# Graph network layer on one core: the blend of the experts moved into the stage of the sparse table

## What is computed

```
x = x + experts(layernorm(x))          # 4 experts, gates g[node, e], two of four not zero
    # out = sum_e g[node, e] * (gelu(x @ W1[e] + b1[e]) @ W2[e] + b2[e])
y = layernorm(x)                       # mean and variance of each node's row of 256
h_self, h_neigh = y @ W_self, y @ W_neigh
h_sparse = maxk(h_neigh, 32)           # keep the 32 largest of each row, zero the rest
x = x + h_self + mean over incoming edges of h_sparse[src]
```

## Time and profile before

| what | us |
|---|---|
| median of 3 runs | 4285.53 |
| lowest and highest | 4283.12, 4290.53 |
| the profiled execution's own time | 4285.15 |
| its span in the trace | 4283.4 |
| the stage of the gates, first to last VectorE instruction | 2853.7 to 2879.7 |
| the stage of the blend | 2880.6 to 2947.9 |
| the stage of the sparse table | 2949.6 to 3138.9 |
| busy share over the span: PE, DVE, ACT, POOL | 85%, 63%, 41%, 65% |

### The profile page before, as it was taken

One profiled execution on the slowest core, in us unless ns is written; L12 is line 12 of the kernel. 1 busy time (PEld: TensorE's weight loads), 2 busy tenths in 40 slices (PEclk: granted clock), 3 DMA queues, 4 the chain that ended last, 5 costly groups with the idle time before them and its releaser, 6 DMA issues. The chain is left out here.

```text
span 4283.4 us, 74278 instructions
## 1 busy us (share of the span) xinstructions
PE 3654.7 (85%) x19739; PEld 2736.6 (64%) x19739; DVE 2717.2 (63%) x9603; ACT 1744.8 (41%) x4053; POOL 2802.9 (65%) x2913
## 2 busy tenths in 40 slices
PE   5999977777687889886899999968769999996988
PEld 2565544444455557645788888866358888885667
DVE  7866757666544444336455555568978888886862
ACT  4766644333233233324444544436523333333420
POOL 6777667777777777771777777751667767675330
PEclk9999997888899999865899999989879999998988
DMA  8665553333444443531433333346389999993001
GB/s 285 205 208 200 203 179 113 112 110 113 123 129 131 132 120 105 165 104 22 102 70 66 71 66 70 68 115 212 119 301 384 368 364 385 362 383 125 1 1 60
DMA packets 362257, 690.88 MB, mean 161 GB/s; under 512 B 70066, under 2 KB 188224, under 8 KB 355485
## 3 DMA queue, kind: packets, MB, share of 16 engines
q0 software_dynamic: 133184, 338.60, 26.8%
q1 hardware_dynamic: 228671, 347.51, 24.0%
HBM read 572.74 MB, written 113.14 MB: 160 GB/s over the span
## 5 line engine op out<-in xcount | busy, mean ns | idle before, releaser
L1199 POOL DMA_INDIRECT e_ring<-table,erow x1040 | 1001.7, 963 | 316.9 <-issue 172.2
L1650 PE MATMUL e_sums<-e_ring,e_onehot 128*128 128x257 f32 x2080 | 772.1, 476 | 297.0 <-DMA e_ring<-table,erow 250.8
L2749 POOL DMA_INDIRECT t_source<-source_rows,t_index x632 | 605.6, 958 | 206.6 <-issue 157.8
L1650 PEld LDWEIGHTS e_sums<-e_ring,e_onehot 128*128 128x128 f32 x2080 | 363.1, 216 | 528.2 <-issue 288.9
L1762 POOL DMA_INDIRECT e_ring<-table,esrc x544 | 532.4, 979 | 215.9 <-issue 124.7
L1165 ACT ACTIVATE k_sign<-ramp,low 128x128 bf16<-128x128 f32 x1024 | 361.3, 394 | 436.5 <-PE e_sums L1604 417.5
L1847 PE MATMUL e_total<-e_loads,e_times 128*128 128x256 f32 x3072 | 505.4, 301 | 21.1 <-DMA e_loads<-table 16.7
L645 POOL DMA_INDIRECT r_ring<-rows,esrc x400 | 381.2, 953 | 156.4 <-issue 77.8
L1745 ACT ACTIVATE e_times<-e_tally 128x320 fp32r<-128x320 f32 (+4 forms) x640 | 259.8, 426 | 491.4 <-PE e_tally L1831 486.5
L1847 PEld LDWEIGHTS e_total<-e_loads,e_times 128*128 128x128 f32 x3072 | 411.8, 191 | 70.1 <-issue 29.8
L2933 PE MATMUL t_raw<-big,t_w 128*128 128x256 f32 x1600 | 375.8, 389 | 19.2 <-ACT t_hidden L2768 18.6
(11 more groups left out here) (570 smaller groups left out, 6600.2 us busy)
## 6 DMA issues: line engine op xcount, KB each, us to landing
e_loads<-table SPq DMA_DIRECT2D x512, 256.0 KB
table<-stage SPq DMA_DIRECT2D x49, 1024.0 KB
outputs<-first_outputs SPq DMA_DIRECT2D x49, 512.0 KB, 6.5
first_outputs<-t_stage SPq DMA_DIRECT2D x96, 256.0 KB
t_near<-near_rows SPq DMA_DIRECT2D x79, 256.0 KB
e_ring<-table,erow POOLq DMA_INDIRECT x1040, 2.8
table<-n_split SPq DMA_DIRECT2D x49, 256.0 KB, 2.1
t_source<-source_rows,t_index POOLq DMA_INDIRECT x632, 2.5
```

Source lines behind the costliest of these rows:

```text
L1199: eng.indirect_dma_start(ring[:, t % RING, 0:D], None, table, bass.IndirectOffsetOnAxis(ap=b.erow[:, EARLY + t:EARLY + t + 1], axis=0)).th ...
L1650: eng.matmul(sums[g % SUMS][:, 0:ACCW], onehot[t % ONEHOTS][:, :], ring[:, t % RING, :], start=(t % GROUP == 0), stop=(t % GROUP == GROUP ...
L2749: eng.indirect_dma_start(source[s][:, q, :], None, a.source_rows, bass.IndirectOffsetOnAxis(ap=index[s][:, q:q + 1], axis=0)).then_inc(gat ...
```

## The change

What was the phase `blend` is done inside `sparse_table`; the phase is gone.

- The outputs of the experts land in the big buffer (10 windows instead of 13), as do the diagonal matrices (4 windows) and a new tile `raised` (2 windows). The gates' tile and the fetch semaphores belong to a larger scope, which is now a `Phase` itself, and so ends with a clearing of semaphores and a meeting of the engines.
- All four experts go through TensorE: `lay` makes four diagonal matrices on ScalarE, `blend` does four products, `lift` copies the bank to `raised` on ScalarE, `merge` adds it to the features on GpSimd.
- The first six windows are blended ahead of the first product. In round w of the sparse table stand `lay(w+9)` and `lift(w+8)` on ScalarE, `blend(w+8)` on TensorE, `merge(w+8)` on GpSimd; rounds 0 and 1 take two windows each, and from round 41 there is nothing left to blend.
- The statistics are made by groups of four windows. Groups 0 and 1 stand ahead of the search. Those of group m+2 are a generator whose steps are taken after the MATCH_REPLACE8 of the rounds 1 to 3 in the search of group m: four `bn_stats`, then three, three and one small instructions, the reciprocal, the product.
- ScalarE takes the square root of group k ahead of `norm(4k)`, and `norm(4k)` waits for that group's scale and shift.
- The big buffer is cleared in eight pieces on GpSimd, in rounds 41 to 48.
- `weigh` does two heads in each of the rounds 41 to 44, and `cooling` comes after the last full group.

The core of the diff:

```diff
-FETCHED = 13
+FETCHED = 10
...
-def blend(nc, b, a):
...
+    blended_at = [[6, 7], [8, 9]] + [[w + AHEAD] for w in range(2, NW - AHEAD)] + [[] for _ in range(AHEAD + 1)]
...
 # gpsimd
+            def merge(w):
+                eng.wait_ge(lifted, w + 1)
+                eng.tensor_tensor(b.x[:, w, :], b.x[:, w, :], raised[w % RAISED][:, :], ALU.add).then_inc(blended, 1)
...
+            for w in range(FIRST):
+                merge(w)
             for w in range(NW):
+                for ahead in blended_at[w]:
+                    merge(ahead)
+                if w >= CLEARED:
+                    empty(w - CLEARED)
                 eng.wait_ge(evacuated, w + 1)
+                eng.wait_ge(counted, w + 1)
                 eng.tensor_tensor(b.x[:, w, :], b.x[:, w, :], full[w % WAYS][:, 0, :], ALU.add).then_inc(added, 1)
                 if w >= LATER:
                     choose(w - LATER)
...
 # vector
+            def statistics(k):
+                cols = slice(GROUP4 * k, min(GROUP4 * (k + 1), NW))
...
+                for w in range(cols.start, cols.stop):
+                    eng.wait_ge(blended, w + 1)
+                    eng.bn_stats(b.counts[:, w, :], b.x[:, w, :]).then_inc(counted, 1)
+                    yield
+                eng.wait_ge(counted, cols.stop)
+                s.did(eng.tensor_tensor(work[:, 0, cols], even(1), odd(1), ALU.add))
+                s.did(eng.tensor_tensor(work[:, 1, cols], even(1), odd(1), ALU.subtract))
+                s.did(eng.tensor_tensor(work[:, 2, cols], even(2), odd(2), ALU.add))
+                yield
...
+                yield
+                s.settled()
+                s.did(eng.tensor_tensor(spread[:, cols], work[:, 2, cols], work[:, 3, cols], ALU.add))
+                yield
+                eng.wait_ge(rooted, k + 1)
+                r.did(eng.reciprocal(b.rstd[:, cols], std[:, cols]))
+                yield
+                r.settled()
+                r.did(eng.scalar_tensor_tensor(b.shift[:, cols], b.mean[:, cols], -1.0, b.rstd[:, cols], ALU.mult, ALU.mult))
...
                         eng.match_replace(left[q][:, :], best[q][:, :], values(q), TAKEN).then_inc(picked[q], 1)
+                        if r > 0:
+                            next(beside, None)
...
-                search(here(0))
+                search(here(0), statistics(2 * i + 2))
...
 # scalar
             def norm(w):
                 wait_if(eng, transposed, w - 1)
+                if w % GROUP4 == 0:
+                    eng.wait_ge(scaled, 2 * (w // GROUP4 + 1))
...
+            def lay(w):
+                wait_if(eng, summed, w - GATES + 1)
+                for e in range(EXPERTS):
+                    gate = eng.activation(gates[w % GATES][:, e, :], b.ident[:, :], ACT.Copy, scale=b.gate[:, w, e:e + 1])
+                gate.then_inc(laid, 1)
+
+            def lift(w):
+                eng.wait_ge(summed, w + 1)
+                wait_if(eng, blended, w - RAISED + 1)
+                eng.activation(raised[w % RAISED][:, :], mixed[w % BANKS][:, 0:D], ACT.Copy).then_inc(lifted, 1)
...
             for w in range(NW):
                 if w + 2 < NW:
+                    if (w + 2) % GROUP4 == 0:
+                        root((w + 2) // GROUP4)
                     norm(w + 2)
                 if w + 1 < NW:
                     copy(w + 1)
+                    for ahead in blended_at[w + 1]:
+                        lay(ahead)
                 if w >= LATER:
                     hide(w - LATER)
                 eng.wait_ge(multiplied, w + 1)
...
                                ACT.Copy).then_inc(evacuated, 1)
+                for ahead in blended_at[w]:
+                    lift(ahead)
```

More of the change, by code:

```diff
@@ L3086, in _ @@
             step(eng.reciprocal(stat[:, 1, :], stat[:, 0, :]))
-            step(eng.tensor_tensor(a.gate[:, :, :], score[:, :, :],
+            step(eng.tensor_tensor(b.gate[:, :, :], score[:, :, :],
                                    stat[:, 1, :].unsqueeze(2).broadcast_to([P, NW, EXPERTS]), ALU.mult))
-def blend(nc, b, a):
[L3099 to L3169, removed]
@@ L3221, in sparse_table @@
         work = sb("n_work", [P, 4, NW])
+        spread = sb("n_spread", [P, NW])
         std = sb("n_std", [P, NW])
@@ L3334, in search @@
                         eng.match_replace(left[q][:, :], best[q][:, :], values(q), TAKEN).then_inc(picked[q], 1)
+                        if r > 0:
+                            next(beside, None)
+                for _ in beside:
+                    pass
                 for w, q in few:
@@ L3351, in pair @@
                         head(w)
-                search(here(GROUP4))
+                search(here(GROUP4), statistics(2 * i + 3) if 2 * i + 3 <= NW // GROUP4 else iter(()))
                 for w in range(WAYS * i, WAYS * i + GROUP4):
                     head(w)
-            s = Chain(eng, stated)
-            variances(eng, s, b, b.counts, work)
             eng.memset(upper[:, 0:D].bitcast(I32), UPPER).then_inc(bounded, 1)
-            eng.wait_ge(rooted, 1)
-            r = Chain(eng, scaled)
-            r.did(eng.reciprocal(b.rstd[:, :], std[:, :]))
-            r.settled()
-            r.did(eng.scalar_tensor_tensor(b.shift[:, :], b.mean[:, :], -1.0, b.rstd[:, :], ALU.mult, ALU.mult))
+            for k in range(2):
+                for _ in statistics(k):
+                    pass
             eng.wait_ge(bounded, 1)
@@ L3420, in weigh @@
                 eng.matmul(bias[:, h * SG:(h + 1) * SG], b.ones[0:1, :], bslice[:, :], start=False, stop=True).then_inc(weighed, 1)
+            for w in range(FIRST):
+                blend(w)
             eng.wait_ge(loaded, 32)
@@ L3425, in _ @@
                 body(w, w % 2)
-                if WEIGHED <= w < WEIGHED + SH:
-                    weigh(w - WEIGHED)
+                for ahead in blended_at[w]:
+                    blend(ahead)
+                if 0 <= w - WEIGHED < SH // 2:
+                    weigh(2 * (w - WEIGHED))
+                    weigh(2 * (w - WEIGHED) + 1)
         @block.scalar
@@ L3456, in _ @@
             copy(0)
+            for w in range(GATES, FIRST):
+                lift(w)
+            for w in blended_at[0]:
+                lay(w)
             for w in range(NW):
                 if w + 2 < NW:
+                    if (w + 2) % GROUP4 == 0:
+                        root((w + 2) // GROUP4)
                     norm(w + 2)
@@ L3504, in attention_phase @@
             attention_edges(nc, b, m, a)
-            a.outputs = [eb(f"outputs{s}", [P, EXPERTS, D]) for s in range(FETCHED)]
-            a.fetched = [ctx.semaphore(f"fetched{s}") for s in range(FETCHED)]
             gates(nc, b, m, a)
-            blend(nc, b, a)
 SB = INNER // P
```

118 lines of the change are left out of this document (90 added, 28 removed).

## The result

The changed kernel takes 4298.0 us (median of 8, 4292.3 to 4305.8) against 4286.3 for the kernel before: a ratio of 1.0028, 95% interval 1.0019 to 1.0038, or +12 us (8 to 16). Predicted was 4301. Its profiled execution took 4292.33 us (span 4290.5), the lowest of its eight.

What follows compares the result with a forecast made beforehand. The blend was taken as bound by TensorE, the sparse table by VectorE. Terms -49.4 + 0.85 + 22 + 12 + 30 = +15.5 us on a median of 4285.5 gave 4301; forecast 4290 to 4310 (0.50), range 4264 to 4322.

Steps and rivals of the forecast that it cites:

- The opening: From the stage's start to the first MATCH_REPLACE8: 33.4 us instead of 83.6, start 0.8 later, 49.4 us gained.
- The larger scope's meeting: New meeting of the engines at the end of the larger scope: takes 0.85 us back.
- The rest of the stage: After the first replacement: statistics 22 us, GpSimd collisions 12 us and new wait 30 us added.
- The statistics: Statistics instructions on VectorE inside the searches: 2.1 us a group, 1.1 for the last, 22 us in all.
- The collisions: VectorE's small statistics instructions slowed beside GpSimd's additions: 0 to 2.4 us a group, 1.2 taken, 12 us in all.
- the six with two inputs in SBUF: Of the nine small statistics instructions, the six expected to exclude GpSimd's reads, 0.76 us beside it against 0.16 alone.
- The wait: VectorE's fourth head after each search waits for a ScalarE and GpSimd chain from the shift: 3.1 us a group, 30 in all.
- rival (a): No wait behind the search, as the hide gets through earlier: 4271 us, 4259 without collisions too; chance 0.22.
- Rival (b): The wait is there but small instructions fall between GpSimd's bursts, no collisions: +3.5, 4289 us; chance 0.14.
- rival (c): ScalarE and TensorE become the pace, rounds of more than 4.5 us instead of 3.7: +40, 4325 us; chance 0.14.
- weigh and cooling only move: Attention-logit products and cooling, placed in other rounds late in the stage, were given no cost in the sum.
- The clearing: Eight clearing pieces make GpSimd's rounds 41 to 48 3.4 us against VectorE's 3.3: nothing to 1 us.

Runs made afterwards that it cites:

- all five edits: Changed kernel with lay behind lift, merge behind select, statistics' steps earlier, two intermediate results in PSUM, one head weighed a round: 4255.1 us, 0.9925 of the kernel before.
- one head a round and the steps early: Changed kernel with the statistics' steps taken earlier in the search and one head weighed in each of rounds 41 to 48: 0.9969 of the kernel before.

## Why the prediction was right, point by point

- **The opening: right.** 2964.18 - 2879.36 = 84.8 us before and 2912.81 - 2878.09 = 34.7 after, 50.1 gained for 49.4 predicted: the stage began 0.4 later, not 0.8, and the opening itself was 33.0, not 33.4. The intermediate marks hold too: norm(0) 13.6 us behind the first matrix (13.7 predicted), the fourth product's end 31.7 (32.2). The prediction's steps do not quite add up: from product 0 at 17.0, the paces 1.73 and 1.94 give 31.5. The half clock was there as well, granted 0.50 from the first product at 2881.19 to 2884.7. The paces of two old stages added up to the schedule of a new one. The larger scope's meeting, priced at 0.85, isn't seen: from the last heads to the next phase 11.8 us before (3127.08 to 3138.86) and 11.4 after.
- **The rest of the stage: right**, +65.2 (162.9 before, 228.1 after, first replacement to last heads) for 22 + 12 + 30 = 64.
- **The statistics: right.** With all five edits a cycle has no wait and no collision and is 15.19 us against 13.16 without statistics: 2.03 a group, 2.1 predicted. The estimate of 3.1 from the Trainium skill (VectorE: DVE Perf Modes, the TRN2 errata) added up durations, and that sum does not hold here: the durations of neighbours overlap (0.15 long, 0.07 apart at 3017.18), and the spacing is what counts.
- **The collisions: right in size, wrong in which instructions.** What is left of the 65.2 after 21.4 of statistics (ten sets at 2.03, and the last at the 1.1 predicted), 28.1 of waits ahead of heads and searches and 3.5 in group 10 is 12, 1.2 a group. In groups 2 to 8 it is 19.5 - 13.16 - 3.0 - 2.03 = 1.35. But I counted the six with two inputs in SBUF, and L3303 with one input is among the slowest. A row of the kernel before, 1.5 us behind the last of rows 6 and beside an instruction of GpSimd, already showed it, three times the 0.17 of its like at 3906.09:

```profile
3913.30 0.49 DVE L3649 TENSOR_SCALAR mean<-l_work 128x7 f32<-128x7 f32 x1
```

The Trainium skill (SBUF — State Buffer, Who interferes with whom) counts tensor_scalar from SBUF to SBUF too, in a two-port mode, and limits only the case of two inputs in SBUF to instructions of GpSimd that read. The runs agree with both: with their inputs in PSUM the two took 157 and 148 ns against 447 and 322, the tensor_scalar beside the MEMSET took 1.06 us, and in the version with all five edits the sums, with two inputs in SBUF, stand inside a MEMSET and are not held:

```profile
3062.29 1.44 POOL L3255 MEMSET big<- 128x1606 f32 x1
3062.38 0.17 DVE L3303 TENSOR_TENSOR n_upper<-counts 128x4 f32<-128x4 f32 x1
3062.45 0.16 DVE L3304 TENSOR_TENSOR n_work<-counts 128x4 f32<-128x4 f32 x1
```

- **The wait: right.** 24.9 us at the fourth heads (26 predicted) and 3.2 for the evacuations in group 1's search (4.0). That the chain starts at the shift and runs through the links named was tested by shortening it in three places: 1.2, 0.9 and 2.1 us less of wait for 1.2, 1.1 and 2.1 us of chain by the expectations. So rival (a) falls by its rows.
- **Rival (b)** falls by the collisions, **rival (c)** by ScalarE's idle time ahead of the root, 4.0 us in the cycle shown and 3.3 or more in every other of groups 1 to 9: I had given it 2.5.
- **"weigh and cooling only move": wrong for weigh.** This step failed, in group 10: VectorE waits 3.1 us for the root and 0.4 for an evacuation where I had nothing. A round of TensorE with two heads has 2.3 us more, and in three such rounds the product runs at 1.2 GHz (3.2 to 3.4 us for 1.88). It is rival (c) for one group. Cooling did only move: its 2 us lie in the last search now, in group 10 before.
- **The clearing: too low.** 0 to 1 us predicted; without it groups 9 and 10 are 2.5 us shorter together (the stage 1.7, with an opening that was 0.8 longer). The term came from the length of GpSimd's rounds; the rows show another cost, pieces that hold up small instructions of VectorE for 1.06 us in one profiled execution and 2.07 across an addition and a piece in the other.

The 3.5 us of group 10 stand against 1.9 too much for the waits, 0.7 for the statistics, 0.7 for the opening and 1.3 for the meeting; they nearly cancel, and that is luck. The +12 of the medians against +15 in the stage is within the interval of the ratio.

## What to carry to other kernels

When a step moves between the steps of a bound engine, price its instructions, but price first the chain that starts at its result and look where in program order the bound engine meets the end of that chain: here 28 of 65 us were a wait that no engine's load explains, and making the result 2.1 us earlier took back 19 without removing any work. Work that "only moves" has to be laid into the round that it moves to: two heads a round were 5 us dearer than one. And once the wait is gone the gain of the change shows: the same merged stage, reordered, is 26 us shorter than the two it replaces.

## What the runs showed of the hardware

- A tensor_scalar of four columns from SBUF to SBUF lasts 0.15 us. Where an instruction of GpSimd had begun first, it lasted until that one's end, 0.37 or 0.70 beside additions and 1.06 beside a MEMSET, which reads nothing; behind an addition with a MEMSET next, 2.07. With its input in PSUM it lasted 0.14 to 0.16 there too.
- A tensor_tensor with both inputs in SBUF lasted up to 0.77 beside additions of GpSimd, and 0.16 and 0.17 inside a MEMSET. A reciprocal of four columns lasted 0.15 to 0.18 throughout, nine times beside additions in the version with all five edits.
- The replacement behind a tensor_scalar that is held lasted 1.10 instead of 0.41 (3095.94), while the one ahead of it, inside the same MEMSET, lasted 0.40 (3095.33). So its own access isn't held; it waits its turn.
- The first product of TensorE behind ScalarE's wait for the shift took 2.7 to 3.7 us in five of the seven cycles from 2943 to 3070 of the changed kernel (granted clock 0.54 to 0.72), 1.97 and 1.98 in the other two (1.00), and 1.88 in all 21 products between. TensorE had idled 3.0 to 3.9 us ahead of each, in the two that stayed at 2.4 GHz as well (3.1): such an idle stretch can bring 1.2 GHz, and need not.
- In group 10 three products, one a round, ran at 1.2 GHz. Between them 2.4 GHz was granted (1.00 from 3096.5 to 3099.5 and from 3104.0 to 3106.3), and two of the three came without idle time, behind two heads' small products. With one head a round and the steps early, the product at 3075.40, behind 1.4 us of idle time, took 3.26, and the four behind it took 1.88 (granted 1.00 from 3080 to 3095). What in the two heads' products brings the clock down is not shown.
